# Two fp4 quantization ladders interleaved on VectorE in an adaLN transformer block

## The reference

```python
def fp4_quant_dequant(x):
    xb = x.reshape(shape[:-1] + (shape[-1] // 16, 16))
    scale = jnp.max(jnp.abs(xb), axis=-1, keepdims=True) / 6.0
    scale = jnp.maximum(scale, jnp.float32(1e-12))
    xn = xb / scale
    idx = jnp.searchsorted(_MID, jnp.abs(xn))
    q = _GRID[idx] * jnp.sign(xn) * scale
def fp4_linear(x, w):
    return einsum('bsk,nk->bsn', fp4_quant_dequant(x), fp4_quant_dequant(w))
...
h = silu(fp4_linear(x, w_gate)) * fp4_linear(x, w_up)
return fp4_linear(h, w_down)
...
h = layernorm(x) * (1 + ca) + sa
x = x + ga * attn(h)
h = layernorm(x) * (1 + cb) + sb
x = x + gb * ffn(h)
```

## Time and profile before

| | |
|---|---|
| median of 2 runs | 4380.13 us (4372.35 to 4387.92) |
| the profiled execution | 4353.82 us, its span 4352.3 us |
| spans of the 8 cores | 4329.0 to 4352.3 us |
| VectorE busy | 2852.7 us, 66% |
| TensorE matmul busy | 2324.8 us, 53% |
| ScalarE busy | 1195.2 us, 27% |
| granted TensorE clock, mean of the core | 0.758 |
| shares of the chain that ended last | VectorE 48%, TensorE 19%, VectorE's queue 11%, DMA 8%, ScalarE 5% |

### The profile page before, as it was taken

One profiled execution on the slowest core, in us unless ns is written; L12 is line 12 of the kernel. 1 busy time (PEld: TensorE's weight loads), 2 busy tenths in 40 slices (PEclk: granted clock), 3 DMA queues, 4 the chain that ended last, 5 costly groups with the idle time before them and its releaser, 6 DMA issues.

```text
span 4352.3 us, 33486 instructions; the slowest of 8 cores (4329.0 to 4352.3 us)
## 1 busy us (share of the span) xinstructions
PE 2324.8 (53%) x9132; PEld 864.5 (20%) x9132; DVE 2852.7 (66%) x4120; ACT 1195.2 (27%) x1236; POOL 201.6 (5%) x324
## 2 busy tenths in 40 slices
PE   7746665878878787866635620002232355323227
PEld 7712211322222222211100100001111122111113
DVE  0056666319999999999932439997777642777761
ACT  0001111068989898977600000000000000000000
POOL 0001111000110111000000000000000000000000
PEclk9978777899999898988855655556666678666658
DMA  7421112312222222222220120001111112111102
GB/s 226 130 62 42 45 52 73 92 44 59 68 70 57 73 73 68 63 69 66 57 88 1 39 39 7 12 15 29 32 29 32 39 32 85 32 29 32 29 24 87
DMA packets 260933, 239.51 MB, mean 55 GB/s; under 512 B 193040, under 2 KB 229264, under 8 KB 256656
## 3 DMA queue, kind: packets, MB, share of 16 engines
q1 hardware_dynamic: 233360, 122.27, 11.0%
q0 software_dynamic: 27392, 115.11, 8.9%
HBM read 157.36 MB, written 46.66 MB: 47 GB/s over the span
## 4 chain that ended last, share of the span: by engine, by line
DVE 48%; PE 19%; DVEq 11%; DMA 8%; issue 6%; ACT 5%; SPq 1%; POOL 0%; ACTq 0%; POOLq 0%
PE dp_ps L1057 4%; ACT pb L734 3%; PE mod_ps L259 3%; DVEq L193 3%; PE bc L798 3%; DVE lad_w L199 3%; PE v_ps L578 3%; DVE x_own L199 2%; DVEq L146 2%; DMA wu_sb<-wuts 2%; DVE lad_w L222 2%; DVE lad_g L219 2%; DVE lad_ab L194 2%; DVE lad_bm L182 2%; DVEq L201 2%
## 5 line engine op out<-in xcount | busy, mean ns | idle before, releaser
L734 ACT ACTIVATE pb<-s_ps,negc 128x1024 bf16<-128x1024 f32 x1024 | 1038.6, 1242 | 115.0 <-PE s_ps L706 114.1
L1001 PE MATMUL g_ps<-wg_sb,h2q 128*128 128x512 bf16 (+1 forms) x768 | 211.6, 442 | 1189.3 <-DMA wu_sb<-wuts 1059.0
L702 PE MATMUL s_ps<-qb,kb 64*128 64x512 bf16 x1024 | 393.8, 387 | 186.6 <-ACT pb L734 117.8
L717 PE MATMUL pv_ps<-pb,vres 128*65 128x512 bf16 x992 | 414.3, 418 | 84.8 <-DVE O L768 84.8
L706 PE MATMUL s_ps<-qb,kb 64*128 64x512 bf16 x1024 | 406.8, 400 | 0.0
L723 PE MATMUL pv_ps<-pb,vres 128*65 128x512 bf16 x992 | 389.0, 392 | 0.0
L1019 ACT ACTIVATE silu_sb<-g_ps 128x1024 bf16<-128x1024 f32 (+1 forms) x56 | 47.1, 842 | 1195.0 <-PE u_ps L1011 1195.0
L1001 PEld LDWEIGHTS g_ps<-wg_sb,h2q 128*128 128x128 bf16 x768 | 86.6, 116 | 1310.7 <-issue 1256.2
L154 ACT ACT_TABLE_LOAD x5 | 6.4, 1283 | 955.8 <-DMA h2q<-h2qt 326.9
L460 PE MATMUL qk_ps<-h,wqk 128*128 128x512 bf16 x768 | 211.4, 425 | 36.6 <-ACT qkst L472 21.6
L1024 DVE TENSOR_TENSOR hmul<-silu_sb,u_ps 128x1024 bf16<-128x1024 bf16 (+1 forms) x56 | 55.6, 993 | 266.5 <-ACT silu_sb L1019 260.6
(11 more groups left out here) (164 smaller groups left out, 3659.7 us busy)
## 6 DMA issues: line engine op xcount, KB each, us to landing
wmod<-wmod POOLq DMA_DIRECT2D x8, 3072.0 KB, 14.0
x_own<-x SPq DMA_DIRECT2D x2, 8192.0 KB, 55.0
x_own<-wgate POOLq DMA_DIRECT2D x22, 512.0 KB, 4.7
x_own<-wup POOLq DMA_DIRECT2D x22, 512.0 KB, 4.8
x_own<-wdown POOLq DMA_DIRECT2D x16, 704.0 KB, 6.3
wd<-wdts SPq DMA_DIRECT2D x88, 128.0 KB, 2.1
wg_sb<-wgts SPq DMA_DIRECT2D x10, 1024.0 KB, 5.5
wu_sb<-wuts SPq DMA_DIRECT2D x10, 1024.0 KB, 7.9
```

The costliest lines, as they stand in the source:

```text
L702: em("tensor", lambda e, kt=kt, qoff=qoff, pb=pb, sAB=sAB: e.matmul(sAB[:, 0:512], kbuf[pb][0:64, P * kt:P * (kt + 1)], qbuf[pb][0:64, qof ...
L717: em("tensor", lambda e, ktp=ktp, qs2p=qs2p, gp=gp, h0=h0: e.matmul(pv_ps[0][:, 512 * qs2p:512 * (qs2p + 1)], vres[:, ktp, 65 * h0:65 * (h ...
L734: exp_at[g] = em("scalar", lambda e, sAB=sAB, pAB=pAB: e.activation(pAB[:, 0:1024], sAB[:, 0:1024], AF.Exp, bias=negc[:], scale=0.125), mA)
L1001: em("tensor", lambda e, kc=kc, qt=qt, iw=iw, tb=tb, tbase=tbase, off=off: e.matmul(g_ps[tb][:, off:off + iw], h2q[:, kc, tbase + P * qt:t ...
```

## The change

`emit_quant` is split. `quant_stages` returns the 14 groups as lists of instructions, on a part of the scratch tiles that begins at `lo`. `emit_quant` runs one such list with a drain behind each group, as before. The new `emit_quant_pair` runs two of them side by side: group by group, first the instructions of the one, then those of the other, then one drain for both. The scratch tiles of the two phases are twice as wide, `h2a` has two buffers, an unused tile is gone.

The layernorm phase goes over 8 pairs of tiles: each scaling instruction for both, then a wait for the transposes out of both `h2qt` buffers, the paired quantization, one marker and two transposes. In the feed-forward phase a step ends with its product; its quantization is put on a list, and when the list holds two, `flush_q` emits the paired quantization, one marker, and the transposes of both steps. A slice has an even number of steps, so the list is empty at each slice's end. The weights' quantization beside the attention still goes one at a time.

```diff
-        def emit_quant(x_ap, out_ap, F):
+        def quant_stages(x_ap, out_ap, F, lo=0):
...
+            return [
+                [lambda e: e.tensor_reduce(bm, x3, AX, ALU.max,
+                                           apply_absolute_value=True)],
+                [lambda e: e.reciprocal(s6, bm)],
...
+        def emit_quant(x_ap, out_ap, F, lo=0):
+            V = blk.vector
+            for stage in quant_stages(x_ap, out_ap, F, lo):
+                for op in stage:
+                    V(op)
+                V(lambda e: e.drain())
+
+        def emit_quant_pair(xa, oa, Fa, xb, ob, Fb):
+            V = blk.vector
+            for sa_, sb_ in zip(quant_stages(xa, oa, Fa, 0),
+                                quant_stages(xb, ob, Fb, Fa)):
+                for op in sa_:
+                    V(op)
+                for op in sb_:
+                    V(op)
+                V(lambda e: e.drain())
...
-            make_ladder(p5, 1024)
+            make_ladder(p5, 2048)
...
-            for tt in range(NT):
-                tb = tt % 2
...
+            for tp in range(NT // 2):
+                tts = (2 * tp, 2 * tp + 1)
...
+                for tb in range(2):
+                    for tk in tq_done[tb]:
+                        wtt("vector", tk)
+                emit_quant_pair(h2a[0][:], h2qt[0][:], D, h2a[1][:], h2qt[1][:], D)
...
-            make_ladder(p6, 1024)
+            make_ladder(p6, 2048)
...
-            dtmp = sb("dtmp", [P, 512], F32, p6)
...
+                    def flush_q():
+                        if not pend_q:
+                            return
+                        if len(pend_q) == 2:
+                            (t0, Wa, _, _, _), (t1, Wb, _, _, _) = pend_q
+                            emit_quant_pair(hmul[t0][:, 0:Wa], hmul[t0][:, 0:Wa], Wa,
+                                            hmul[t1][:, 0:Wb], hmul[t1][:, 0:Wb], Wb)
...
+                        v_hq = em("vector", lambda e: e.memset(
+                            smallf[0:1, 61:62], 0.0), mV)
+                        wt("sync", mV, v_hq)
+                        for tb_, W2_, io_, iw_, qts_ in pend_q:
+                            tdma[tb_] = [dmaT("sync",
...
-                            emit_quant(hmul[tb][:, 0:W2], hmul[tb][:, 0:W2], W2)
...
+                            pend_q.append((tb, W2, io, iw, qts))
+                            if len(pend_q) == 2:
+                                flush_q()
+                    flush_q()
```

More of the change, by code:

```diff
@@ L173, in make_ladder @@
                 LAD[nm] = sb("lad_" + nm + sfx, [P, QF], BF16, stack)
-        def emit_quant(x_ap, out_ap, F):
+        def quant_stages(x_ap, out_ap, F, lo=0):
             L = LAD
             NB = F // 16
-            V = blk.vector
+            b0 = lo // 16
             x3 = x_ap.rearrange("p (b k) -> p b k", k=16)
             o3 = out_ap.rearrange("p (b k) -> p b k", k=16)
[L181 to L228, removed]
@@ new lines, in quant_stages @@
+            ab3 = L["ab"][:, lo:lo + F].rearrange("p (b k) -> p b k", k=16)
+            bm, s6, rc = (L[n][:, b0:b0 + NB] for n in ("bm", "s6", "rc"))
+            ab, w1, w2, w3, w4, g2 = (L[n][:, lo:lo + F] for n in
+                                      ("ab", "w1", "w2", "w3", "w4", "g2"))
+            rcb = L["rc"][:, b0:b0 + NB, None].broadcast_to([P, NB, 16])
+            s6b = L["s6"][:, b0:b0 + NB, None].broadcast_to([P, NB, 16])
+            return [
+                [lambda e: e.tensor_reduce(bm, x3, AX, ALU.max,
+                                           apply_absolute_value=True)],
+                [lambda e: e.reciprocal(s6, bm)],
+                [lambda e: e.tensor_scalar(rc, s6, 6.0, 1e12, ALU.mult, ALU.min)],
+                [lambda e: e.reciprocal(s6, rc),
+                 lambda e: e.scalar_tensor_tensor(ab, x_ap, -1.0, x_ap,
+                                                  ALU.mult, ALU.max)],
+                [lambda e: e.tensor_tensor(ab3, ab3, rcb, ALU.mult)],
+                [lambda e: e.tensor_scalar(w1, ab, 0.25, 0.5, ALU.is_gt, ALU.mult),
+                 lambda e: e.tensor_scalar(w2, ab, 0.75, 0.5, ALU.is_gt, ALU.mult),
+                 lambda e: e.tensor_scalar(w3, ab, 1.25, 0.5, ALU.is_gt, ALU.mult),
+                 lambda e: e.tensor_scalar(w4, ab, 1.75, 0.5, ALU.is_gt, ALU.mult)],
+                [lambda e: e.tensor_tensor(w1, w1, w2, ALU.add),
+                 lambda e: e.tensor_tensor(w3, w3, w4, ALU.add),
+                 lambda e: e.tensor_scalar(g2, ab, 2.5, 1.0, ALU.is_gt, ALU.mult)],
+                [lambda e: e.tensor_tensor(w1, w1, w3, ALU.add),
+                 lambda e: e.tensor_scalar(w2, ab, 3.5, 1.0, ALU.is_gt, ALU.mult),
+                 lambda e: e.tensor_scalar(w4, ab, 5.0, 2.0, ALU.is_gt, ALU.mult)],
+                [lambda e: e.tensor_tensor(g2, g2, w2, ALU.add)],
+                [lambda e: e.tensor_tensor(w1, w1, g2, ALU.add)],
+                [lambda e: e.tensor_tensor(w1, w1, w4, ALU.add)],
+                [lambda e: e.scalar_tensor_tensor(g2, x_ap, 0.0, w1,
+                                                  ALU.is_ge, ALU.mult)],
+                [lambda e: e.scalar_tensor_tensor(w1, g2, 2.0, w1,
+                                                  ALU.mult, ALU.subtract)],
+                [lambda e: e.tensor_tensor(
+                    o3, w1.rearrange("p (b k) -> p b k", k=16), s6b, ALU.mult)],
+            ]
@@ L867, in build @@
             nmr2 = sb("nmr2", [P, NT], F32, p5)
-            h2a = sb("h2a", [P, D], BF16, p5)
+            h2a = [sb(f"h2a{i}", [P, D], BF16, p5) for i in range(2)]
             h2qt = [sb(f"h2qt{i}", [P, D], BF16, p5) for i in range(2)]
@@ L980, in build @@
                     pi = [0]
+                    pend_q = []
+                    def flush_q():
[5 more added lines that the diff above has]
+                                            hmul[t1][:, 0:Wb], hmul[t1][:, 0:Wb], Wb)
+                        else:
+                            t0, Wa, _, _, _ = pend_q[0]
+                            emit_quant(hmul[t0][:, 0:Wa], hmul[t0][:, 0:Wa], Wa)
+                        v_hq = em("vector", lambda e: e.memset(
[3 more added lines that the diff above has]
+                            tdma[tb_] = [dmaT("sync",
+                                              hq[:, io_ // P:io_ // P + iw_ // P,
+                                                 P * qt:P * (qt + 1)],
+                                              hmul[tb_][:, iw_ * j:iw_ * (j + 1)].rearrange(
+                                                  "p (c q) -> p c q", q=P))
+                                         for j, qt in enumerate(qts_)]
+                        pend_q.clear()
                     for ii, (io, iw) in enumerate(isl_bounds):
```

31 lines of the change are left out of this document (13 added, 18 removed).

## The result

The changed kernel takes 4417.9 us (median of 11 runs) against 4361.4 us for the kernel before (10 runs by now). The ratio is 1.0147, 95% interval 1.0109 to 1.0185: 64 us slower, 48 to 81 (the two medians are 56.5 us apart). The forecast was 79 us slower than a base of 4380 us, 4459 us in all; the measured time lies in the range of 4415 to 4495, 3 us above its low end, and within 2% as was thought likeliest. The profiled execution took 4437.3 us, span 4435.8 us on core 2.

A forecast was written before the change was run, and what follows sets the result against it. VectorE's instructions, SyncE's queue at a slice's end and the first step after it were taken to bound the kernel. Gate/up +93.1 us and layernorm -13.9 gave +79 us on 4380.1: 4459 us, range 4415 to 4495.

The forecast's parts named there:

- What bounds: Gate/up phases: time is set by VectorE's instructions, SyncE's queue at a slice's end and the first step after it.
- The head: Start of each wide slice: paired quantization waits for the second product, VectorE stands 5.6 us, 56.0 us in ten.
- The transposes' wait: Pair boundary within a slice: second product waits for hmul's transposes until 6.6 us after marker M; 50.7 us wide, 19.8 narrow.
- The queue: SyncE at a wide slice's end: two more transposes ahead of the weight loads, 2.54 us, ten times 25.4 us.
- Layernorm phase: Layernorm phase: 0.8 us wait left per pair, seven times; 6.9 us added, 20.8 us saved, net -13.9 us.
- The drains: VectorE's quantization: shared drains save 2.03 us per pair, 2.34 us with the marker, 65.5 us over 28 gate/up pairs.
- The base: Whole kernel: median 4380.1 us of the runs shown, to which the forecast's 79 us were added.
- Longer landings: Rival, pair's four transposes: the last lands 3.6 to 4.2 us after issue, +29 us, 4488 us; chance 0.32.
- The queue time: Rival, VectorE's quantization: sequencer time held up by drains is half hidden by pairing, 104 us, giving 4355 us; chance 0.05.
- drains are not free: Against the rival that VectorE flushes after every instruction anyway, so 76 us of savings fall away, 4535 us; chance 0.02.

The follow-up runs named there:

- the kernel with the first pair: Changed kernel with four hmul buffers and each slice's last two steps quantized alone, so slices begin on a pair: 4353.2 us, ratio 0.9983 to the kernel before.
- four buffers: Changed kernel with four hmul buffers in place of two: 4353.9 us, ratio 0.9985 to the kernel before.

## Why the prediction was right, and where its sizes were off

*What bounds.* Right. The three things named (VectorE's row, SyncE's queue at a slice's end, the first step after it) are the ones that the experiments move one by one. The direction and the 2% held for the reason given.

*The head*, 5.6 us a wide slice: the hole is 5.69 us, 5.60 us of it more than the usual gap. Held, and shown apart by the kernel with the first pair (53 of 56 us in the wide slices). It holds at the full clock, see the last section.

*The transposes' wait*, second product at M + 6.6 us: it is M + 6.63. That it is so close is partly luck, as the fourth transpose starts 0.10 us later than I had it (M + 4.10) and the answer takes 0.09 us and not 0.2. In total 70.5 us expected, 74.3 us in the waits, 64 us (by the ratios 71) taken away by four buffers.

*The queue*, 2.54 us: 6.04 - 3.36 = 2.68 us, and 2.8 us by the ten holes. The transposes issue 1.28 to 1.31 us apart in the changed kernel, not 1.27.

*Layernorm phase.* The hole left over is 0.93 us (0.8 expected). The phase gained 16.4 us, not 13.9.

*The drains* are the term that was mis-sized. I priced one at 0.07 + 0.08 us from two spacings of 0.69 us instructions, and with the marker came to 2.34 us per pair. In the profile after it is 2.40 + 0.22 = 2.62 us, and drains put back cost 0.171 us each. The 0.28 us missing in 28 pairs are 8 us. A pair of the layernorm phase saves about 3.0 us and not 2.6 (38.2 to 38.3 us from reduction to reduction with a wait that costs some 0.9 us, against 2 x 20.17 us before): 3 us more in 8 pairs. With both the sum would have been 79 - 11 = 68 us; the profiles show 70 and the timing 64. The two spacings themselves give 0.76 - 0.60 = 0.16 us; I had split this into two halves rounded down. The 14th gap of a quantization, which the 13 leave out, I had counted with the marker. Instructions of other lengths save a little more: the two reciprocals take 1.26 us to the next stage with a drain between them and 1.04 without.

*The base.* I set the forecast on the median 4380 of two runs; ten runs have 4361. That is 19 of the 41 us between 4459 and 4418, the savings above are 11, and the remaining 11 are inside the interval of the ratio. On the median of the ten runs the same 79 us would have given 4440 us. That the measured time is still inside the range owes something to its low end, which allowed for savings by unseen overlap.

*Rivals.* Longer landings did not come (2.4 us median, longest 2.9). The queue time did not go with the drains, and drains are not free. The Trainium skill's rule in "VectorE: DVE Perf Modes", section "The DRAIN you can't avoid", that chaining gains nothing, doesn't carry over to drains written as instructions: here they cost 0.171 us each. The page compares copies with and without semaphores between them, and no run here tests that, so it is my transfer of the rule that fails and not the page's measurement.

## What to carry to other kernels

Before independent work is interleaved to share a barrier, price what the grouping delays: the start of the group waits for its last input, its outputs leave together and late, and every buffer is released one group later. Here 2.6 us saved per pair stood against 5.6, 5.1 and 2.7 us for the late start, the buffers and the late outputs. Groups that leave the first and the last step of a stage alone, with one more set of output buffers, give up one pair in each slice, keep the saving of the others and pay none of the three. And a load that nothing in its queue has to precede is worth moving to another queue, here an idle one: that alone gave 224 us.

## What the runs showed of the hardware that was not expected

The head cost depends on TensorE's clock, which was no part of the time before in a wide slice beyond its first step. In the profiled execution with four buffers the second step's matmuls on core 6 and on core 2, with the granted clock of that stretch and the product that waits (columns of the third row: stretch, length, busy time and count of each engine, granted clock, DMA share, GB/s):

```profile
3071.43 3.62 PE L1035 MATMUL g_ps<-wg_sb,h2q 128*128 128x512 bf16 x16
3074.89 3.62 PE L1045 MATMUL u_ps<-wu_sb,h2q 128*128 128x512 bf16 x16
```

```profile
3071.00:3078.00 7.00, 7.00 (x34) 3.19 (x33) 1.22 (x1) 1.02 (x1) 0.00 (x0) 1.00 0.00 0
```

```profile
3079.87 1.22 DVE L1058 TENSOR_TENSOR hmul<-silu_sb,u_ps 128x1024 bf16<-128x1024 bf16 x1 [5.69 <-ACT silu_sb L1053]
```

```profile
3092.15 4.38 PE L1035 MATMUL g_ps<-wg_sb,h2q 128*128 128x512 bf16 x16
3096.35 4.38 PE L1045 MATMUL u_ps<-wu_sb,h2q 128*128 128x512 bf16 x15
```

```profile
3092.00:3099.00 7.00, 6.91 (x28) 2.85 (x28) 1.22 (x1) 1.02 (x1) 0.00 (x0) 0.81 0.00 0
```

```profile
3102.09 1.22 DVE L1058 TENSOR_TENSOR hmul<-silu_sb,u_ps 128x1024 bf16<-128x1024 bf16 x1 [7.18 <-ACT silu_sb L1053]
```

Core 6 is granted the full 2.4 GHz, sixteen matmuls start 3.46 us after the sixteen before, and VectorE waits 5.69 us. Core 2 is granted 0.81, and not as a mix of full and half speed in turn: each of the seven microseconds by itself shows 0.81. The same sixteen come 4.20 us after, and VectorE waits 7.18 us. Before the change these matmuls lay under a quantization. So pairing made the kernel more sensitive to the clock. The kernel before can't show this by itself, because all its cores were granted 0.64 to 0.67 over the wide slices of each half. The kernel whose slices begin on a pair can: on cores 2 and 3 the heads of the first half (granted 0.65) are 5.68 us and the five of the second half (granted 0.59) are 7.18 us each, and their ten wide slices take 1042 and 1043 us where the other cores take 1025 to 1030 us. In the kernel whose slices begin with single steps two cores were granted 0.61 and 0.62 in the second half, and their ten wide slices take 1004.9 and 1005.5 us where the others take 1001.2 to 1004.3 us. (These clocks are means over 2960 to 3480 us and 3700 to 4180 us.) The changed kernel has such heads too: two of the ten on each of cores 2 and 3 are 7.18 us.
